# Maxima of two heads at once on the two halves of TensorE's array, projections two steps later

## What is computed

```python
# attention of one sample: 8 heads of 16 channels, 512 positions
q, k, v = proj(layernorm(x), Wq, bq), proj(ctx, Wk, bk), proj(ctx, Wv, bv)
scores = einsum('bhqd,bhkd->bhqk', q, k) / sqrt(16)
attn = softmax(scores, axis=-1)
x = x + tanh(g_xattn) * einsum('bhqk,bhkd->bhqd', attn, v)   # back to channels by positions
# then, per token (4096 of them, 512 wide): rmsnorm(layernorm(x)), router over 8 experts,
# top 2, expert FFNs (512 -> 256 -> 512, silu gate) and one shared FFN
x = x + tanh(g_ffn) * (moe + shared)
```

## Time and profile before

| | |
|---|---|
| three runs | 1458.8, 1460.76, 1463.73 us; median 1460.76 |
| the profiled execution | 1463.89 us, its span 1462.1 us |
| PE (TensorE) busy | 96% of the span |
| DVE (VectorE) | 68% |
| ACT (ScalarE) and POOL (GpSimd) | 59% each |
| attention part | from about 28 us to 962 us |
| expert part | from there to the end |

### The profile page before, as it was taken

The page is one execution under the profiler, slowest core; times in us unless marked ns, Lnnn a source line. Parts: engine busy times, 40 slices in busy tenths (PEclk is TensorE's granted clock), DMA queues, the critical chain, the costliest instruction groups (busy, mean ns, idle before and its releaser), DMA issues.

```text
span 1462.1 us, 25166 instructions
## 1 busy us (share of the span) xinstructions
PE 1396.7 (96%) x7290; PEld 720.9 (49%) x7290; DVE 997.4 (68%) x2172; ACT 866.0 (59%) x1720; POOL 862.8 (59%) x1276
## 2 busy tenths in 40 slices
PE   5899999999999999999999999989999999999997
PEld 1222333333333333333333333258788888888886
DVE  5777888888798888888888888846654333333332
ACT  2477777777677777777777777744333433333332
POOL 6536766766677677777777765435211555555553
PEclk9899999999999999999999999999999999999999
DMA  5857767767676778778677776256653789886565
GB/s 142 202 132 192 200 178 186 196 176 191 167 196 173 195 188 195 180 182 206 169 195 192 177 171 161 83 184 149 149 188 90 171 205 223 189 193 113 107 113 80
DMA packets 183329, 247.93 MB, mean 170 GB/s; under 512 B 31045, under 2 KB 105420, under 8 KB 183198
## 3 DMA queue, kind: packets, MB, share of 16 engines
q1 hardware_dynamic: 160846, 208.42, 54.1%
q0 software_dynamic: 18256, 37.38, 13.8%
q10 hardware_dynamic: 4096, 0.53, 0.3%
HBM read 141.85 MB, written 103.88 MB: 168 GB/s over the span
## 4 chain that ended last, share of the span: by engine, by line
PE 62%; DMA 13%; issue 11%; DVE 5%; POOL 3%; ACT 3%; SPq 1%; POOLq 1%; ACTq 1%; DVEq 0%
PE bank L1382 19%; PE bank L1339 13%; PE bank L1310 10%; PE bank L1288 10%; DMA pv_d<-arena 4%; DMA arena<-m_rows 4%; PE bank L1273 3%; PE bank L1315 2%; DVE row_max L860 2%; POOL xs L748 2%; PE bank L1326 2%; DMA arena<-pv_d 2%; ACT arena L1130 1%; PE bank L1277 1%; DMA out<-xs,ids 1%
## 5 line engine op out<-in xcount | busy, mean ns | idle before, releaser
L860 DVE TENSOR_REDUCE row_max<-bank 128x1 f32<-128x512 f32 x1024 | 674.3, 683 | 110.0 <-PE bank L1288 92.4
L1130 ACT ACTIVATE arena<-bank 128x512 f32<-128x512 f32 x1024 | 563.9, 611 | 243.6 <-PE bank L1310 211.4
L1288 PE MATMUL bank<-arena 96*128 96x512 bf16 x1024 | 397.1, 390 | 21.7 <-DVE row_max L860 14.2
L1310 PE MATMUL bank<-arena 98*128 98x512 bf16 x1024 | 390.7, 384 | 10.4 <-DMA arena<-m_rows 6.4
L1339 PE MATMUL bank<-arena 128*32 128x512 f32 x2048 | 275.3, 610 | 1.0 <-ACT arena L1130 0.7
L760 POOL DMA_INDIRECT out<-xs,ids x71 | 112.8, 1588 | 171.4 <-ACT xs L1214 139.6
L1288 PEld LDWEIGHTS bank<-arena 96*128 96x128 bf16 x1024 | 100.9, 99 | 189.4 <-DVE row_max L860 103.7
L1310 PEld LDWEIGHTS bank<-arena 98*128 98x128 bf16 x1024 | 102.9, 101 | 180.1 <-ACT arena L1130 77.5
L1382 PE MATMUL bank<-w_ring,h_hi 128*128 x568 | 183.1, 403 | 0.0
L1203 ACT ACTIVATE arena<-bank 128x256 f32<-128x256 f32 x103 | 39.5, 384 | 186.2 <-PE bank L1382 182.2
L649 POOL TENSOR_TENSOR arena<-arena 128x512 bf16<-128x512 f32 x62 | 71.5, 1153 | 122.5 <-ACT arena L1122 120.1
(11 more groups left out here) (174 smaller groups left out, 1992.2 us busy)
## 6 DMA issues: line engine op xcount, KB each, us to landing
arena<-parts_q SPq DMA_DIRECT2D x64, 256.0 KB
pv_d<-arena SPq DMA_DIRECT2D x32, 512.0 KB, 6.9
w_ring<-split_d SPq DMA_DIRECT2D x60, 256.0 KB
parts_k<-arena SPq DMA_DIRECT2D x96, 128.0 KB
arena<-parts_k SPq DMA_DIRECT2D x32, 384.0 KB
parts_q<-arena SPq DMA_DIRECT2D x96, 128.0 KB
arena<-in_w SPq DMA_DIRECT2D x36, 256.0 KB, 5.5
arena<-in_ctx SPq DMA_DIRECT2D x32, 256.0 KB, 3.1
```

The lines of the kernel that those rows point to most:

```text
L860: nc.vector.reduce_max(row_max[b % 2][:, u:u + 1], m_ps[(STEPS * b + u) % M_BANKS][:], AX_X).then_inc(s_mx, 1)
L1130: nc.scalar.activation(probs[group % 3][:, j, :], e_ps[n % E_BANKS][:], ACT.Exp, scale=float(DH) ** -0.5).then_inc(s_exp, 1)
L1288: nc.tensor.matmul(m_ps[n % M_BANKS][:], q_stack[b % 3][0:STACK, h, qt * P:(qt + 1) * P], k_stack[b % 3][0:STACK, h, :], start=True, stop= ...
L1310: nc.tensor.matmul(e_ps[n % E_BANKS][:], k_stack[b % 3][0:SHIFTED, h, kt * P:(kt + 1) * P], q_stack[b % 3][0:SHIFTED, h, :], start=True, s ...
```

## The change

Maxima are made from three part products instead of six, and two at once. The stack of 16-row copies now has 112 rows. Rows 0 to 47 hold one triple of part products, rows 64 to 111 the other triple, and rows 48 to 63 ones against two rows of maxima and zeros. Heads 2a + j of a group (a = 0, 1) have the leading triple (`FIRST`) at row 64 a and the rest (`SECOND`) at the other half, so that a maxima product of an a = 0 head uses the array's upper half of rows and one of an a = 1 head the lower half. An exp product runs over all 112 rows.

- `max_scores` is called at even steps only. It issues two matmuls, one for each half, into two banks, and waits until at most one older maximum is open. `maximum` waits at even steps for both products of a pair, and puts its result where the head order wants it.
- The parts lie in DRAM as (part, row, head, position), in an order that lets more parts be read in one run. Reads are now per half, 12 DMAs per batch (six for keys, six for queries), in runs of two heads (2 KB).
- The blank middle rows (32 to 63) of the query stacks are zeroed and those of the key stacks set to ones before the first reads: one set by VectorE ahead of its first moments, two by GpSimd, the queries' ahead of its first `normalise`, the keys' behind it. The first three reads of keys wait for that (`s_blank`).
- Projections, their evacuations and casts, the token turn and the logits are one or two steps later; `COUNT_SLOT` is 30.

```diff
-K_PARTS = (HI, MID, LO, HI, MID, HI)
-Q_PARTS = (HI, HI, HI, MID, MID, LO)
+STORED = ((LO, MID, HI), (HI, MID, LO))
+FIRST = ((MID, HI, HI), (HI, HI, MID))
+SECOND = ((LO, MID, HI), (HI, MID, LO))
...
+READS = 2 * sum(len(stored_runs(parts, n)) for parts in (FIRST, SECOND) for n in range(2))
+STACK = 3 * DH
+LANE = P // 2
+SHIFTED = LANE + STACK
...
-PROJECT_AT = {22: (3, 0), 26: (3, 1), 7: (2, 2)}
-EVAC_AT = {23: (3, 0), 27: (3, 1), 8: (2, 2)}
-HIGH_AT = (25, 29)
+PROJECT_AT = {24: (3, 0), 28: (3, 1), 8: (2, 2)}
+EVAC_AT = {25: (3, 0), 29: (3, 1), 9: (2, 2)}
+HIGH_AT = (27, 31)
...
-TURN_TOKENS_AT = 10
-LOGITS_AT = 14
+TURN_TOKENS_AT = 12
+LOGITS_AT = 16
...
+        def middle_rows(stack):
+            return stack[LANE // 2:LANE, :, :].rearrange("p h l -> p (h l)").bitcast(F32)
+
+        def lane(v, a):
+            return v.rearrange("p (g a j) l -> p a g (j l)", g=2, a=2)[:, a, :, :]
...
+                if b < 3 and n == 0:
+                    sp.wait_ge(s_blank[b], 2)
...
-                for at, part, k in runs(order):
-                    sp.dma_start(stack[at * DH:(at + k) * DH, :, :],
-                                 src[:, part:part + k].rearrange("h t d l -> (t d) h l")
-                                 ).then_inc(s_rd[b % 3], DMA)
+                for a in range(2):
+                    for row, parts_at in ((LANE * a, FIRST), (LANE * (1 - a), SECOND)):
+                        for at, part, k in stored_runs(parts_at, n):
+                            sp.dma_start(lane(stack[row + at * DH:row + (at + k) * DH, :, :], a),
+                                         lane(src[part:part + k].rearrange("t d h l -> (t d) h l"), a)
+                                         ).then_inc(s_rd[b % 3], DMA)
...
             def maximum(b, u):
-                dve.wait_ge(s_ms, STEPS * b + u + 1)
+                if u % 2 == 0:
+                    dve.wait_ge(s_ms, STEPS * b + u + 2)
...
             def max_scores(b, u):
...
-                if n >= M_BANKS:
-                    pe.wait_ge(s_mx, n - M_BANKS + 1)
-                nc.tensor.matmul(m_ps[n % M_BANKS][:], q_stack[b % 3][0:STACK, h, qt * P:(qt + 1) * P],
-                                 k_stack[b % 3][0:STACK, h, :], start=True, stop=True).then_inc(s_ms, 1)
+                if n + 1 >= M_BANKS:
+                    pe.wait_ge(s_mx, n + 1 - M_BANKS + 1)
+                for a in range(2):
+                    rows, h = slice(LANE * a, LANE * a + STACK), GROUP * g + 2 * a + j
+                    nc.tensor.matmul(m_ps[(n + a) % M_BANKS][:], q_stack[b % 3][rows, h, qt * P:(qt + 1) * P],
+                                     k_stack[b % 3][rows, h, :], start=True, stop=True).then_inc(s_ms, 1)
...
-                    if is_b(i + 1):
+                    if s % 2 == 0 and is_b(i + 1):
                         max_scores(i + 1, s)
```

More of the change, by code:

```diff
@@ L41, in runs, with stored_runs @@
     return out
-READS = len(runs(K_PARTS)) + len(runs(Q_PARTS))
-STACK = len(K_PARTS) * DH
-SHIFTED = STACK + 2
+def stored_runs(parts, n):
+    return runs([STORED[n].index(part) for part in parts[n]])
+READS = 2 * sum(len(stored_runs(parts, n)) for parts in (FIRST, SECOND) for n in range(2))
+STACK = 3 * DH
+LANE = P // 2
+SHIFTED = LANE + STACK
 STEPS = HEADS * KT
-PROJECT_AT = {22: (3, 0), 26: (3, 1), 7: (2, 2)}
-EVAC_AT = {23: (3, 0), 27: (3, 1), 8: (2, 2)}
-HIGH_AT = (25, 29)
+PROJECT_AT = {24: (3, 0), 28: (3, 1), 8: (2, 2)}
+EVAC_AT = {25: (3, 0), 29: (3, 1), 9: (2, 2)}
+HIGH_AT = (27, 31)
 MAX_AT = (18, 2)
@@ L83 @@
 EXP_SLOT = 26
-COUNT_SLOT = 29
+COUNT_SLOT = 30
 TAKEN = -3.0e38
@@ L257, in build @@
         pv_ps, misc_ps = banks[6:8]
-        parts_d = [[dram(f"parts_{n}{i}", (HEADS, 3, DH, L), BF16) for i in range(2)] for n in "kq"]
+        parts_d = [[dram(f"parts_{n}{i}", (3, DH, HEADS, L), BF16) for i in range(2)] for n in "kq"]
         pv_d = dram("pv_d", (HEADS, 2 * DH, L), F32)
@@ L273, in build @@
         s_ones = sem("s_ones")
+        s_blank = [sem(f"s_blank{i}") for i in range(3)]
         s_x = [sem(f"s_xin{i}") for i in range(4)]
@@ L440, in write @@
                     sp.wait_ge(s_part, 4 * b + 2 * n + part)
-                sp.dma_start(parts_d[n][b % 2][:, part, :, :], parts[n][part]).then_inc(s_wr[n], DMA)
+                sp.dma_start(parts_d[n][b % 2][STORED[n].index(part)].rearrange("d h l -> h d l"), parts[n][part]
+                             ).then_inc(s_wr[n], DMA)
             def read(b, n):
@@ L707, in scatter @@
                         meta[:, k, b, :], None).then_inc(s_sc2, DMA)
+            pool.wait_ge(s_iota, 7)
+            for n in (1, 2):
+                nc.gpsimd.memset(middle_rows(q_stack[n]), 0.0).then_inc(s_blank[n], 1)
+                pool.wait_ge(s_blank[n], 1)
             normalise(0)
-            for v, k in zip(v_ones[1:], k_stack[1:]):
-                link(nc.gpsimd.memset(v[:, :, :, DH:], 1.0))
-                link(nc.gpsimd.memset(ones_rows(k), TWO_ONES))
+            for n in (1, 2):
+                link(nc.gpsimd.memset(v_ones[n][:, :, :, DH:], 1.0))
+                nc.gpsimd.memset(middle_rows(k_stack[n]), TWO_ONES).then_inc(s_blank[n], 1)
+                pool.wait_ge(s_blank[n], 2)
             for i in TURNS:
@@ L856, in maximum @@
             def maximum(b, u):
-                dve.wait_ge(s_ms, STEPS * b + u + 1)
+                if u % 2 == 0:
+                    dve.wait_ge(s_ms, STEPS * b + u + 2)
                 if u == 0 and b >= 2:
                     dve.wait_ge(s_mt, 2 * (b - 2) + 2)
-                nc.vector.reduce_max(row_max[b % 2][:, u:u + 1], m_ps[(STEPS * b + u) % M_BANKS][:], AX_X).then_inc(s_mx, 1)
+                half, w = divmod(u, GROUP * KT)
+                at = GROUP * KT * half + GROUP * KT // 2 * (w % 2) + w // 2
+                nc.vector.reduce_max(row_max[b % 2][:, at:at + 1], m_ps[(STEPS * b + u) % M_BANKS][:], AX_X).then_inc(s_mx, 1)
             def maxima_rows(b, half):
@@ L1281, in max_scores @@
             def max_scores(b, u):
-                h, qt = divmod(u, KT)
+                g, w = divmod(u // 2, GROUP * KT // 2)
+                j, qt = divmod(w, KT)
                 n = STEPS * b + u
@@ L1306, in exp_scores @@
                 if n == 0:
-                    pe.wait_ge(s_ones, 2)
+                    pe.wait_ge(s_ones, 1)
                 if n >= E_BANKS:
```

8 lines of the change are left out of this document (3 added, 5 removed).

## The result

| | before | after |
|---|---|---|
| median (range) of four runs, side by side | 1462.24 us (1458.80 to 1464.59) | 1571.78 us (1563.96 to 1575.05) |
| ratio, 95% interval | | 1.074 (1.070 to 1.079) |
| span of the profiled execution | 1462.1 us | 1562.1 us |
| first and last exp product | 50.57 and 961.26 us | 54.93 and 1060.18 us |
| mean granted clock | 0.991 | 0.955 |

The change costs 110 us, where 49 were forecast: slower, as said, but beyond the upper end of the range (1550). Of the 100 us between the two spans 94.6 lie between the first and the last exp product, 4.4 before the first, and 1 in the expert part. The page of the kernel after answers to the earlier trace rows: TensorE (PE) is no longer busy nearly always, and less of the chain of waits is its own work, 43% of the span.

What follows compares the result with a forecast made beforehand. The loop through the denominators' reciprocal was taken to bind: 30.2 us a turn against 28.4, over 29 turns +52, startup -1, last two turns -1, so +50: 1514 profiled, 1510 by the runs' median; range 1425 to 1550.

Steps and rivals of the forecast that it cites:

- The bound and its loop: VectorE's reciprocal at step 13 waits for the denominators' DMA; that loop, already 28.0 us, sets the turn and grows to 30.2.
- Rivals 2 and 4: Denominators in time: 2, TensorE sets a 27.3 us turn, 1427, chance 0.21; 4, also free shape changes, 1381, 0.07.
- rivals 3 and 4: Row halves cost no shape change: 3, loop stands, 1484, or 1458 with low landings (chance 0.12); 4, no loop, 1381, 0.07.
- The sum of the loop: Reciprocal to reciprocal after the change: 12.7 + 7.2 + 2.8 + 7.5 = 30.2 us a turn.
- First stretch: Loop from the reciprocal to the write of the keys' high part: 12.7 us against 10.24 before.
- Reads: Six key reads instead of three on SP, ahead of the values' store: 2.8 us against 1.4, bounds 2.5 and 3.0.
- Landings: Write of the keys' high part to the reads 7.2 us; values' store and denominators' load to the reciprocal 7.5.
- halves not at once: Rival 1: a pair's two products run in turn, 0.22 us more per pair, 31.5 a turn, 1548; chance 0.11.
- Pair 0.22 and change 0.10: TensorE: a pair costs one product, 0.22 us (-3.5 a turn); 24 more shape changes at 0.10 cost +2.4.
- Hand-over 0.9: TensorE waits 0.3 us for row maxima at each of three uncovered pairs, +0.9 us a turn.
- Later steps: Projections, casts, token turn and logits move later; the keys' cast falls behind exp 27, within the loop's first stretch of 12.7.
- Startup -1: Before the loop: VectorE's saved blank fill gives -1.8 us, two more query reads cost 0.9; -1 in all.

Runs made afterwards that it cites:

- e15: Kernel after with ten unused 112-row products filling TensorE's wait before the maxima pair at step 16; 1543.34 us, ratio 1.054.
- e7b: Kernel after with SP's queue reordered (values stored before key reads, reciprocals stored after query reads) and the reciprocal at step 18, not 13; 1454.38 us, ratio 0.995.
- e5: Kernel before with only the change's later steps for projections, casts, token turn, logits and counts; 1528.42 us, ratio 1.047.
- e1: Kernel after with the reciprocal of the denominators at step 21 instead of 13; 1610.73 us, ratio 1.094.
- e4: Kernel before with the reciprocal of the denominators at step 21 instead of 13; 1604.55 us, ratio 1.093.
- e13: Kernel after with eleven unused 48-row products filling TensorE's wait before the maxima pair at step 16; 1584.16 us, ratio 1.079.
- e6: Kernel before with the change's by-row DRAM layout and reads per half (six for keys, eight for queries), old stack and products; 1526.54 us, ratio 1.046.
- e12: Kernel before with the parts by row in DRAM, number and order of reads as before; 1465.41 us, ratio 1.001.
- e14: Kernel before with each read split in two (heads 0 to 3, 4 to 7), layout as before; 1495.46 us, ratio 1.020.

## Why the prediction was right or wrong

- **The bound and its loop: right.** The denominators hold the turn. The reciprocal waits 2.92 us in the turn shown and 2.4 on average, where 1.0 was forecast to grow to about 3; TensorE stands 2.35. Rivals 2 and 4 needed the wait gone and fell with it, rivals 3 and 4 needed changes of shape that cost nothing and fell with the 0.32 behind each pair.
- **The sum of the loop: 1.7 us too short, the step that failed.** *First stretch* 14.4 for 12.7: every product was priced at the full clock, although the forecast itself had TensorE idle 2 to 3 us a turn. At the full clock the sum was right: 12.53 in such turns of e15. So the clock is the term that the prediction put at nothing; e15's mean of 13.0, with 6 turns at the lower clock, gives back 1.4 of the 1.7. *Reads* 4.1 for 2.8: six reads were priced at the 0.47 of reads of another pattern; they take 0.60 to issue, 0.64 with the gap to the next. *Landings* 6.5 for 7.2 and 6.9 for 7.5: values between full and empty queues were taken, and the landings came at or below the empty ones. 1.7 + 1.3 - 0.7 - 0.6 = 1.7. Over 28 turns that is 48 us of the 62 missed. The start adds 5.4, and the median of the kernel after lies 8 us above its profiled execution, where the forecast had taken 3 below; with these 11 the parts come to 2 us more than the miss.
- **Upper end too low.** It took in "halves not at once", a rival that the trace of before did not support, and no lower clock, for which the wait in my own forecast spoke. The earlier trace rows spoke against it: there the same wait brought no fall.
- **Pair 0.22 and change 0.10: right.** 26.4 us of own work a turn in e7b, as summed; the two products of a pair start 3 ns apart (median of the kernel after). The Trainium skill's rule, page "TensorEngine Tiling (Array Packing)", section Key Properties, that a change of tiling mode drains the engine agrees with the 0.32 us from the start of each pair to the next product, 0.10 over the 0.22 without a change.
- **Hand-over 0.9: right for the three pairs priced**, at s = 2, 6 and 22. In e7b 0.6 more stand at pairs that other products were said to cover; why VectorE is late there is open. It did not decide: the loop set the turn.
- **Later steps: the cast's way was right.** They lengthen the first stretch, by 1.2 us at the full clock. That e5 shows 2.5, the sum's whole growth, is luck: e5 has none of the pairs, and its clock falls in nearly every turn. What was missed is that SP has a second loop through the same reciprocal (e1, e4); its price was not in the sum, and in the kernel after it is not the one that binds.
- **Startup -1: wrong**, +4.4. The first exp product starts at 54.93 in place of 50.57. The first maxima start at 29.60 for 27.92. In both kernels they wait for the reads of the queries and not for the fill, so that the 1.8 us saved there brought nothing, and these reads take SP 3.76 us where four took 1.75, more than the 0.9 allowed. The turn of maxima alone is 2.7 us longer: with little beside them TensorE waits 0.8 us for most pairs, which is the hand-over again. Before, then after:

```profile
27.92 4.39 PE L1288 MATMUL bank<-arena 96*128 96x512 bf16 x8 [1.62 <-DMA arena<-parts_q]
```

```profile
31.03 0.61 PE L1315 MATMUL bank<-arena 48*128 48x512 bf16 x2 [0.81 <-DVE row_max L883]
```

Not in the sum either: ScalarE issued a row DMA for 4.83 us once (below), in a turn of 37 us. It is one cause of that turn's first stretch of 20.3 us, which adds 0.2 to the mean of 14.4.

## What to carry to other kernels

Before an engine is made faster, find the loop that spans a turn: here one wait for a small DMA, queued between maxima, held all engines. Another order of one DMA queue, with the reciprocal five steps later, was worth 118 us, where the halved products were worth nothing. Price a forecast wait twice, once for its length and once for the clock that it costs, and price a DMA's issue by its pattern. And see who waits for a step in each queue that it stands in before it is moved: the reciprocal moved "out of the way" cost the kernel before 136 us.

## What the runs showed of the hardware

- With its wait filled by ten products of 112 rows TensorE fell from 2.4 to 1.2 GHz 7 times in 800 us (e15); filled by eleven of 48 rows, which kept it as busy in time, it fell 23 times, and unfilled 25 (e13, the kernel after). The two fills also differ in whether they have the shape of the pair behind them or of an exp product.
- A read of two heads of each group of four from rows of all heads takes SP 0.60 us to issue (e6, the kernel after). Reads in the other patterns take 0.42 to 0.47 (e12, e14, the kernel before).
- A short copy on VectorE took 2.52 us beside two operations of GpSimd, a maximum, which reads PSUM, beside the same engine 0.69. The Trainium skill, page "SBUF — State Buffer", section "SBUF: two separate sides", says that GpSimd and VectorE in some of its operations, such as copies in a mode with two ports, share a pair of ports under an exclusive lock, and that the loser blocks for the whole instruction. The row agrees in that the copy ends when GpSimd's second subtraction does; it spans two of GpSimd's instructions and not one.
- ScalarE's queue took 4.83 us to issue one small DMA, with all exponentials behind it; ScalarE stood 5.08 us. The chain of waits of the kernel after, then ScalarE's timeline:

```profile
621.86 0.18 ACTq L1173
...
622.07 4.83 ACTq L1173
...
627.59 0.61 PE bank L1337
```

```profile
626.94 1.57 ACT L1154 ACTIVATE arena<-bank 128x512 f32<-128x512 f32 x3 [5.08 <-issue]
```

The longest such issue in the kernel before is 1.75 us; why it was so long is open.
